# Nyström attention on one core: another order of the work between the pseudoinverse products, on TensorE, VectorE and ScalarE

## What is computed

```python
k = split_heads(x @ Wk); q = split_heads(x @ Wq) / math.sqrt(HS); v = split_heads(x @ Wv)   # 16 heads of 16
q_l = q.reshape(B, H, M, denom, HS).sum(axis=-2) / denom          # 64 landmarks
k_l = k.reshape(B, H, M, denom, HS).sum(axis=-2) / denom
s1 = softmax(einsum('bhld,bhmd->bhlm', q, k_l))
s2 = softmax(einsum('bhmd,bhnd->bhmn', q_l, k_l))
s3 = softmax(einsum('bhmd,bhld->bhml', q_l, k))
z = s2.T / (col * row)            # col, row: the largest sums of |s2|
for _ in range(6):
    xz = s2 @ z
    z = 0.25 * z @ (13 * I - xz @ (15 * I - xz @ (7 * I - xz)))
out = (s1 @ (z @ (s3 @ v))) @ Wo + bo
```

## Time and profile before

| | us |
|---|---|
| median of 3 runs | 1236.3 |
| lowest and highest | 1235.24, 1238.79 |
| the profiled execution | 1237.7 |
| its span | 1235.9 |
| of that: TensorE busy | 1125.6 (91%) |
| VectorE, ScalarE, GpSimd busy | 750.7, 595.1, 544.3 |

### The profile page before, as it was taken

One profiled execution on the slowest core, in us unless ns is written; L12 is line 12 of the kernel. 1 busy time (PEld: TensorE's weight loads), 2 busy tenths in 40 slices (PEclk: granted clock), 3 DMA queues, 4 the chain that ended last, 5 costly groups with the idle time before them and its releaser, 6 DMA issues.

```text
span 1235.9 us, 29651 instructions
## 1 busy us (share of the span) xinstructions
PE 1125.6 (91%) x11140; PEld 915.5 (74%) x11141; DVE 750.7 (61%) x1391; ACT 595.1 (48%) x953; POOL 544.3 (44%) x634
## 2 busy tenths in 40 slices
PE   7899889999999378899999998989999888999997
PEld 6677678888887266677777776868887677888786
DVE  5536346766665466757668666655445346667664
ACT  5433235666664345354444554525443335666663
POOL 2131544666665624333534342234204535665674
PEclk8899899999999789999999999999999999999999
DMA  7173214222210300000000000011453032221220
GB/s 239 34 263 137 95 49 163 66 69 69 66 56 28 119 19 3 2 3 2 3 2 3 2 4 3 3 36 69 154 188 103 18 120 71 65 63 58 69 68 18
DMA packets 42030, 80.45 MB, mean 65 GB/s; under 512 B 9012, under 2 KB 33719, under 8 KB 40896
## 3 DMA queue, kind: packets, MB, share of 16 engines
q1 hardware_dynamic: 28640, 53.62, 12.3%
q0 software_dynamic: 13280, 25.27, 6.8%
HBM read 57.21 MB, written 27.15 MB: 68 GB/s over the span
## 4 chain that ended last, share of the span: by engine, by line
PE 68%; DVE 16%; ACT 6%; issue 6%; DMA 2%; POOL 1%; another core or an unknown queue 1%; DVEq 0%; ACTq 0%; POOLq 0%; SPq 0%
PE PS L1596 16%; PE PS L1610 10%; PE PS L1522 8%; PE PS L1539 6%; PE PS L1784 4%; PE PS L1677 3%; PE PS L1797 3%; PE PS L1603 3%; DVE A_NM L722 2%; DVE A_NM L729 2%; PE PS L1459 2%; PE PS L1546 2%; PE PS L1747 1%; PE PS L1818 1%; PE PS L1721 1%
## 5 line engine op out<-in xcount | busy, mean ns | idle before, releaser
L1596 PE MATMUL PS<-WHL,XGH 128*128 128x512 f32 x624 | 217.0, 429 | 3.5 <-DVE WHL L604 3.4
L1610 PE MATMUL PS<-WD,XNT 128*128 x624 | 149.9, 383 | 1.5 <-ACT XNT L1063 1.5
L1373 POOL TENSOR_TENSOR A_A<-A_XC,A_ST 128x320 f32<-128x320 f32 (+1 forms) x96 | 73.7, 781 | 172.2 <-ACT A_ST L1129 171.6
L625 DVE SCALAR_TENSOR_TENSOR XNT<-PS,WHO,XNT 128x512 f32<-128x512 f32 x78 | 58.3, 748 | 120.5 <-PE PS L1596 104.1
L1596 PEld LDWEIGHTS PS<-WHL,XGH 128*128 128x128 f32 x624 | 111.3, 189 | 22.6 <-issue 2.7
L1058 ACT ACTIVATE XNT<-PS,WHO 128x512 f32<-128x512 f32 x78 | 53.7, 688 | 148.7 <-PE PS L1596 135.5
L1277 POOL DMA_INDIRECT who_dram<-TOK,SLOT x64 | 66.1, 1033 | 132.7 <-issue 108.7
L1539 PE MATMUL PS<-SDH,HHL 128*128 128x256 f32 x512 | 108.0, 294 | 18.2 <-DVE X L551 15.8
L1610 PEld LDWEIGHTS PS<-WD,XNT 128*128 128x128 f32 x624 | 112.6, 190 | 15.9 <-issue 2.0
L1596 PE MATMUL PS<-WHL,XGL 128*128 128x512 f32 x312 | 123.1, 395 | 0.0
L1282 POOL DMA_INDIRECT X<-xs_dram,WHO x78 | 99.5, 1276 | 51.2 <-issue 26.5
(11 more groups left out here) (256 smaller groups left out, 2548.9 us busy)
## 6 DMA issues: line engine op xcount, KB each, us to landing
xs_dram<-WG SPq DMA_DIRECT2D x16, 512.0 KB, 2.9
WU<-in_r_up SPq DMA_DIRECT2D x2, 4096.0 KB, 13.9
shared_dram<-X SPq DMA_DIRECT2D x16, 512.0 KB, 3.1
WG<-in_r_gate SPq DMA_DIRECT2D x2, 4096.0 KB, 16.9
WD<-in_r_down SPq DMA_DIRECT2D x4, 2048.0 KB
X<-in_x SPq DMA_DIRECT2D x8, 512.0 KB, 9.3
X<-mid_dram SPq DMA_DIRECT2D x8, 512.0 KB, 3.8
X<-xs_dram,WHO POOLq DMA_INDIRECT x78
```

What stands on the lines that cost most here:

```text
L625: dve.scalar_tensor_tensor(B["RH"][:, u * F:(u + 1) * F], banks[3 + u][:], score(t), B["RS"][:, u * F:(u + 1) * F], ALU.mult, ALU.mult).th ...
L1373: pool.tensor_tensor(a, x, st, ALU.add).then_inc(att["a"], 1)
L1596: ins = pe.matmul(banks[bank][:], tok, w[:, k * F:(k + 1) * F], start=(k == 0 and i == 0), stop=(k == KD - 1 and i == 2))
L1610: ins = pe.matmul(banks[7][:, 0:D], B["HT"][:, u * F + f * P:u * F + (f + 1) * P], B["WD"][:, bass.ds(ex * (KF * D) + f * D, D)], start=(f ...
```

## The change

No operation is added or taken away; blocks move between gaps, a few waits and PSUM banks go with them.

- TensorE: `denominators(old)` goes from step 2 to step 0, behind `heads(old, 1)`. In step 2, `turn_nm3` and `project_qk(far, 0)` now lead. `project_v(nxt, 1)` comes ahead of `s1_turned(b, 0)`. `project_qk(far, 1)` stands ahead of the first product of step 4, `project_qk(far, 2)` and `s1_max(nxt, 0)` ahead of the second; the column sums (now the function `column_sums`) and `s1_max(nxt, 1)` go ahead of the first product of step 5, `project_qk(far, 3)` and `turn_sums` ahead of its second. `start_t` comes before `turn_nm1`.
- VectorE: both key landmarks of `far` are reduced at the end of the round, the reciprocal of the denominators comes in step 0, `add_projection(done, 0)` behind `chain_x(b, 1)`, `s1_max(nxt, 0)` ahead of `chain_x(b, 4)`, the second `s1_max` in two halves around `chain_b(b, 5)`, and `start_t` ahead of `chain_x(b, 5)`.
- ScalarE: `numerators` is split, its first half stands ahead of `chain_s(b, 0)`; the copies follow the projections.
- Banks: `project_qk` uses 6, 6, 6, 7 in place of 7, 6, 6, 6; `project_v` 6 and 7 in place of 6 and 6; `turn_nm1` 7 in place of 6; the column sums and `turn_sums` 6 in place of 7.

```diff

@@ -860,8 +861,9 @@
         if b == NG - 1:
             first_rows(1)
         if exists(nxt):
-            landmarks(nxt, 1, 1)
             s3_max(nxt, 0)
+        if exists(old):
...
             key_block(nxt)
@@ -874,28 +876,25 @@
             low_tokens(far, 1)
         if exists(nxt):
             s2_shift(nxt)
+        chain_x(b, 1)
         if exists(done):
             add_projection(done, 0)
-        chain_x(b, 1)
         if exists(nxt):
             s2_sum(nxt)
+        chain_b(b, 2)
         if exists(ln):
             batch_stats(ln)
...
-        if exists(ln):
             batch_aggregate(ln)
...
         if exists(nxt):
             key_rows(nxt)
-        if exists(old):
-            denominators(old)
         chain_x(b, 2)
+        if exists(nxt):
+            row_sums(nxt)
         if exists(far):
             landmarks(far, 0, 0)
-        if exists(nxt):
-            row_sums(nxt)
@@ -912,28 +911,30 @@
             heads_norm(old)
         if exists(nxt):
             row_kept(nxt)
+            s1_max(nxt, 0, (0, 1))
         chain_x(b, 4)
         if exists(nxt):
-            s1_max(nxt, 0)
+            column_max(nxt)
+            s1_max(nxt, 1, (0,))
         chain_b(b, 5)
         if b == NG - 1:
             denominators(b)
         if exists(nxt):
-            s1_max(nxt, 1)
-            column_max(nxt)
+            s1_max(nxt, 1, (1,))
...
             first_scale()
+        if exists(nxt):
+            start_t(nxt)
+        chain_x(b, 5)
         if exists(far):
             landmarks(far, 0, 1)
-        chain_x(b, 5)
+            query_block(far)
+        if exists(nxt):
+            start_y(nxt)
+            product_kept(nxt)
         if exists(far):
-            query_block(far)
             landmarks(far, 1, 0)
-        if exists(nxt):
-            start_t(nxt)
-            start_y(nxt)
-        if exists(nxt):
-            product_kept(nxt)
@@ -1163,9 +1164,11 @@
     for b in PERIODS:
         old, nxt, far, ln = b - 1, b + 1, b + 2, b + 3

+        if exists(old):
+            numerators(old, 0)
         chain_s(b, 0)
         if exists(old):
-            numerators(old)
+            numerators(old, 1)
...
+        chain_s(b, 2)
+        if exists(nxt):
             act.wait_ge(att["nm3_ready"], count("nm3_ready", nxt, 1))
             act.copy(B["NM3T"][:], banks[7][:, 0:P]).then_inc(att["nm3"], 1)
-        chain_s(b, 2)
-        if exists(nxt):
-            exp3(nxt, 0)
         if exists(far):
             projected(far, 0)
+            rounded(far, 0)
+        if exists(nxt):
+            exp3(nxt, 0)
+            values(nxt, 1)
         if exists(b):
             exp1(b, 0)
-        if exists(far):
-            rounded(far, 0)
-        if exists(nxt):
+        chain_s(b, 3)
+        if exists(nxt):
+            sums_kept(nxt, 0)
             act.wait_ge(att["kbd"], count("kbd", nxt, 1))
             act.copy(B["KBDR"][:], B["KBD"][nxt % 2][:]).then_inc(att["bdr"], 1)
-        if exists(nxt):
-            values(nxt, 1)
-        chain_s(b, 3)
-        if exists(nxt):
-            sums_kept(nxt, 0)
             exp3(nxt, 1)
         if exists(b):
             exp1(b, 1)
+        if exists(far):
+            projected(far, 1)
         chain_s(b, 4)
         if exists(far):
-            projected(far, 1)
             rounded(far, 1)
-        if exists(nxt):
-            sums_kept(nxt, 1)
+            projected(far, 2)
+            rounded(far, 2)
...
+        if exists(nxt):
+            sums_kept(nxt, 1)
...
         chain_s(b, 5)
         if exists(far):
-            projected(far, 2)
-            rounded(far, 2)
-        if exists(far):
             projected(far, 3)
             act.wait_ge(att["qbd"], count("qbd", far, 1))
             act.copy(B["QBDR"][:], B["QBD"][:]).then_inc(att["bdr"], 1)
         if exists(nxt):
             act.wait_ge(att["nm1_ready"], count("nm1_ready", nxt, 1))
-            act.copy(B["NM1T"][:], banks[6][:]).then_inc(att["nm1"], 1)
@@ -1838,23 +1843,27 @@
         if exists(old):
             pe.wait_ge(att["ws"], count("ws", old, 1))
             pe.wait_ge(att["e1"], count("e1", old, 4))
-            pe.wait_ge(att["nm1"], count("nm1", b, 1))
-            pe.wait_ge(att["rec"], count("rec", old - 1, 1))
+            pe.wait_ge(att["tm"], count("tm", b, 1))
             heads(old, 0)
         chain_first(b, 0)
         if exists(old):
-            pe.wait_ge(att["tm"], count("tm", b, 1))
+            pe.wait_ge(att["nm1"], count("nm1", b, 1))
             pe.wait_ge(att["xo"], count("xo", old - 2, 2))
             heads(old, 1)
+            if b == 1:
+                pe.wait_ge(s_picks, 5)
+            pe.wait_ge(att["num"], count("num", old, 1))
+            denominators(old)

         chain_second(b, 0)
         if exists(far):
             pe.wait_ge(att["xn"], count("xn", far, GT))
             pe.wait_ge(att["num"], count("num", old, 2))
-            pe.wait_ge(att["tm"], count("tm", b, 1))
+            pe.wait_ge(att["nm1"], count("nm1", b, 1))
             pe.wait_ge(att["qk"], count("qk", nxt, 4))
             turn(far, 0)
-            pe.wait_ge(att["nm1"], count("nm1", b, 1))
+            pe.wait_ge(att["tm"], count("tm", b, 1))
+            pe.wait_ge(att["rec"], count("rec", old, 1))
             turn(far, 1)
@@ -1879,43 +1888,39 @@
...
+            pe.wait_ge(att["rec"], count("rec", old, 1))
             project_v(nxt, 0)
+
+        chain_first(b, 2)
+        if exists(nxt):
             pe.wait_ge(att["xo"], count("xo", done, 1))
+            pe.wait_ge(att["s3m"], count("s3m", nxt, 4))
             turn_nm3(nxt)
-
-        chain_first(b, 2)
+        if exists(far):
+            pe.wait_ge(att["xtl"], count("xtl", far, 2))
+            pe.wait_ge(att["v_sb"], count("v_sb", nxt, 1))
+            if far == 0:
+                pe.wait_ge(s_low, 4)
+            project_qk(far, 0)
         if exists(nxt):
             if b == -1:
                 pe.wait_ge(s_picks, 5)
             pe.wait_ge(att["nm3"], count("nm3", nxt, 1))
             pe.wait_ge(att["s2s"], count("s2s", nxt, 1))
             s3_turned(nxt, 0)
-        if exists(old):
-            if b == 1:
-                pe.wait_ge(s_picks, 5)
-            pe.wait_ge(att["num"], count("num", old, 1))
-            pe.wait_ge(att["xtl"], count("xtl", far, 2))
-            pe.wait_ge(att["v_sb"], count("v_sb", nxt, 1))
-            denominators(old)
-        if exists(far):
-            pe.wait_ge(att["xtl"], count("xtl", far, 2))
+
+        chain_second(b, 2)
+        if exists(nxt):
             pe.wait_ge(att["nm3"], count("nm3", nxt, 1))
-            if far == 0:
-                pe.wait_ge(s_low, 4)
-            project_qk(far, 0)
-
-        chain_second(b, 2)
+            project_v(nxt, 1)
         if exists(b):
             pe.wait_ge(att["nm1"], count("nm1", b, 1))
             pe.wait_ge(att["e3"], count("e3", nxt, 2))
             s1_turned(b, 0)
-        if exists(nxt):
-            pe.wait_ge(att["v_sb"], count("v_sb", nxt, 1))
-            pe.wait_ge(att["rec"], count("rec", old, 1))
-            project_v(nxt, 1)
...
         chain_first(b, 3)
         if exists(nxt):
+            pe.wait_ge(att["qk"], count("qk", far, 1))
             pe.wait_ge(att["v_sb"], count("v_sb", nxt, 2))
@@ -1924,8 +1929,7 @@
             pe.wait_ge(att["e1"], count("e1", b, 2))
             s3_turned(nxt, 1)
         if exists(done):
-            pe.wait_ge(att["qk"], count("qk", far, 1))
-            pe.wait_ge(att["nm3"], count("nm3", nxt, 1))
+            pe.wait_ge(att["v_sb"], count("v_sb", nxt, 2))
             pe.wait_ge(att["xo"], count("xo", done, 1))
             project(done, 1)
@@ -1936,9 +1940,13 @@
             s1_turned(b, 1)
         if exists(nxt):
             pe.wait_ge(att["rsum"], count("rsum", nxt, 1))
+            pe.wait_ge(att["v_sb"], count("v_sb", nxt, 2))
             pe.wait_ge(att["xo"], count("xo", done, 2))
+            turn_rows(nxt)
+        if exists(far):
+            pe.wait_ge(att["tts"], count("tts", nxt, 1))
             pe.wait_ge(att["qk"], count("qk", far, 1))
-            turn_rows(nxt)
+            project_qk(far, 1)
@@ -1949,22 +1957,24 @@
             pe.wait_ge(att["rmax"], count("rmax", nxt, 2))
             spread_rows(nxt)
         if exists(far):
-            pe.wait_ge(att["tts"], count("tts", nxt, 1))
-            pe.wait_ge(att["xtl"], count("xtl", far, 2))
-            project_qk(far, 1)
-
-        chain_second(b, 4)
+            pe.wait_ge(att["qk"], count("qk", far, 2))
+            project_qk(far, 2)
         if exists(nxt):
             pe.wait_ge(att["ot"], count("ot", old, 2))
             pe.wait_ge(att["e3"], count("e3", nxt, 4))
             pe.wait_ge(att["qkr"], count("qkr", nxt, 2))
             pe.wait_ge(att["bdr"], count("bdr", nxt, 2))
             s1_max(nxt, 0)
+
+        chain_second(b, 4)
+        if exists(nxt):
             pe.wait_ge(att["rs"], count("rs", nxt, 1))
             pv(nxt, 1)
-        if exists(far):
```

(27 more changed lines are left out.)

58 lines of the change are left out of this document (32 added, 26 removed).

## The result

The changed kernel takes 1220.63 us (median of four, 1219.25 to 1224.01), the kernel before 1237.55 beside it (1235.24 to 1243.82): ratio 0.9851 [0.9823, 0.9879], or 16.9 us less. On another chip it was 1219.71 against 1238.38, ratio 0.9836 [0.9789, 0.9884]. The profiled execution took 1224.01, with a span of 1222.2.

What follows compares the result with a forecast made beforehand. TensorE was taken to bound the kernel, with only idle time to win; gains of 11.8 + 3.0 + 1.8 - 0.2 - 0.3 + 0.3 = 16.4 us took the median from 1236.3 to 1220, range 1213 to 1231.

Steps and rivals of the forecast that it cites:

- Denominators to step 0: Steps 0 and 1: moving the denominators removes waits of 0.16, 0.46 and 0.34 us, gaining 0.96 a full round.
- Second product of step 1: Step 1: VectorE's path comes 1.0 us earlier, TensorE's 0.80, so at most 0.1 of the 0.19 wait is left.
- `add_projection`: Before step 2's first product: moved behind XC on VectorE, it gains 0.19 us, with 0.1 to spare.
- `project_v(nxt, 1)`: Step 3: its copy, put ahead of `exp1(b, 0)` on ScalarE, removes the 0.49 us wait before `pv`.
- `project_qk(far, 1)`: Step 4: put ahead of the first product, it covers the 0.66 us wait for `exp1(b, 1)` before `spread_denominators`.
- Step 4: Second product put behind `s1_max(nxt, 0)`, which needs the heads' normalisation: an added wait costing 0 to 0.1 us.
- Step 5: End of the round: VectorE's `start_t` goes ahead of XC and other work, removing TensorE's 0.58 us wait before `start_t`.
- Rival 4: More than counted: round 7's slow clock goes, same-shape blocks side by side save 0.3 us a round; 1216 us, chance 0.09.
- Clock: Round 7's slow stretch, about 1.6 us, counted as staying; it might go (1218.5) or come twice (1221.5).
- the forecast's own case: Nearly all TensorE idle time in full rounds goes; a total of 1216.5 to 1224 us, chance 0.62.
- Rival 1: Waits come back at thin places in steps 1, 2 and 4, losing 8 us of the gain: 1228 us, chance 0.18.
- Rivals 2 and 3: VectorE becomes the bound in steps 4 and 5, 1247 us, chance 0.05; idle is not real slack, 1236, chance 0.06.

Runs made afterwards that it cites:

- the kernel with step 4 put back: Changed kernel with `s1_max(nxt, 0)` behind step 4's second product and its maxima behind `chain_x(b, 4)`: full rounds 48.06 us; 1205.22 us in all, on another chip.
- the kernel with only round 7 altered: Changed kernel with only round 7's denominators back in step 2: round 7 34.64 us, round 6 46.87; 1203.58 us in all, on another chip.
- the undone version: Changed kernel with the denominators back in step 2 in every round: 50.84, 50.82 and 51.24 us in rounds 2 to 4, 49.34 in round 5.
- The experiment with the end of the round: Changed kernel with TensorE's last product, `turn_sums`, `start_y`, `turn_nm1` and `start_t` ordered as before: full rounds 47.97 us, 0.57 more than in the changed kernel.

## Why the prediction was right, and where it was not

The forecast of 1220 stands against 1220.6, and the reason holds: TensorE bounds a full round, its idle time was real slack, and nearly all of it went. That the two totals agree to 1 us is partly luck. The sum hid errors that went both ways: 3.7 us of gain that it left out in the full rounds, and 6.6 us of loss that it left out in round 7 and the fill. The traces account for 13.0 of the 16.9 us. Each term is set against the mean of two executions of each kernel, and then against executions at the same clock, where there are such. By content round 7 lost 0.6 us less and the fill 0.6 more than the table says, since `turn_nm1` changed sides of the cut:

| gain, us | forecast | mean of two | both at clock 1.00 |
|---|---|---|---|
| rounds 2 to 5 | 11.8 | 15.5 | 15.5 |
| round 1 | 3.0 | 3.4 | 3.5 |
| round 0 | 1.8 | 1.1 | 1.85 |
| round 6 | -0.2 | -0.4 | -0.3 |
| round 7 | -0.3 | -3.7 | -0.7 |
| fill | +0.3 | -2.9 | not seen |
| sum | 16.4 | 13.0 | |

For round 7 at clock 1.00 the 33.35 us of the kernel with step 4 put back are set against the 32.61 of before. For round 1 at clock 1.00 the row of the kernel with only round 7 altered is used, whose round 1 is that of the changed kernel (us, TensorE busy, granted clock):

```profile
503.43:550.24 46.81, 44.04 (x898) 1.00 0.01 3
```

**Denominators to step 0 (0.96).** Right, and close to the count. From the first product's start (609.75 in the changed kernel) the second product was forecast at 4.15 and came at 4.00, the reciprocal's end at 5.5 and came at 5.47, XC at 6.4 and came at 6.26. What the count left out is the bank that the later projection shares; the undone version showed that.

**Second product of step 1 (at most 0.1 left of 0.19).** Wrong: all 0.19 stayed. VectorE's low tokens had begun 1.20 us after `turn` ended; now they begin at 616.32, `turn` having ended at 616.03, so 0.29 after: a gain of 0.91, not the 1.0 I took. TensorE's way from `turn` to the product shrank by 0.91 too (4.97 to 4.06, both without the wait), not by the 0.80 of its waits, since its blocks became shorter. A race of two paths that both got shorter by the same amount ends as before.

**`add_projection` (0.19).** Right; the margin is 0.30, not 0.1. I had called it the thinnest place; that is the second product of step 1, which has less than none.

**`project_v(nxt, 1)` (0.49) and `project_qk(far, 1)` (0.66).** Both waits went, alone and together with the rest. Alone the second earned 0.42, since it uncovers 0.39 elsewhere; the forecast had it beside the moves that fill that place.

**Step 4 (0 to 0.1 lost).** Right that nothing is lost, but the term's sign in the full change is a gain: without the move, 0.66 comes back. I had judged it by its own gap and not by the maxima that a later block waits for.

**Step 5 (0.58).** Right. The wait stays away when TensorE's order at the end of the round is put back, so TensorE's order is not what removed it.

**The term that was mis-sized.** The step that failed is "The change removes no work, so idle time is all that it can win in rounds 2 to 5", and with it a full round of 48.2 to 48.5 us and TensorE's busy time "unchanged at 48.1": the round is 47.40, with 47.2 busy. The idle time gave 2.88 a round and the blocks themselves 0.99. Rival 4 named this mechanism with 0.3 us a round. Put together from the starts of neighbouring blocks, less the waits: `turn_nm3` in front of a projection 0.08 where it took 0.28 in front of a waiting 64*64 product, `turn_rows` 0.02 in place of 0.20, `heads(old, 1)` 0.88 in place of 1.06, `start_y` 0.96 for 1.08, the last product 0.96 for 1.04, `project_qk(far, 3)` 1.49 for 1.61, and 0.05 to 0.07 for each of several blocks whose successor had had to wait; against them the column sums take 0.22 more and `project_v(nxt, 0)` 0.08. The first of these as rows of the kernel before and of the changed one:

```profile
624.91 0.27 PE L1707 MATMUL PS<-CB,A_NM 128*128 128x128 f32 x1
625.38 1.32 PE L1784 MATMUL PS<-A_XC 64*64 64x80 f32 x32 [0.19 <-DVE A_XC L818]
```

```profile
624.41 0.33 PE L1709 MATMUL PS<-CB,A_NM 128*128 128x128 f32 x1
624.49 0.48 PE L1679 MATMUL PS<-A_XTH,A_WQH 128*128 128x512 f32 x1
```

625.38 less the wait of 0.19 is 0.28 after the transpose's start; in the changed kernel the projection begins 0.08 after it. The experiment with the end of the round shows the effect by itself (some 0.4 us of its 0.57); for the blocks of the other steps it is read from the two traces, and not tried one by one. Why one neighbour costs more than another is open.

**Clock.** "It may go (1218.5) or come twice (1221.5); I count it as staying" was too kind for the profiled execution. The lower level appeared in four places of the profiled execution: the fill (0.75, against 0.84 before), rounds 0 and 1 (0.96), the end of round 6 (0.96) and round 7 (0.87). In round 7, 0.13 x 37.8 = 4.9 us of full clock are missing, against 0.05 x 34.15 = 1.7 before, so that the round without them is near 33 in both kernels. That is an estimate, as the granted clock is a mean that counts idle time too; measured at 1.00 are 33.35 with the changed order and 32.61 before. The order of the last rounds was forecast well (-0.2 and -0.3; at clock 1.00, with `turn_nm1` counted on one side, -0.3 and -0.1); the clock was not. The Trainium skill, "TensorE: Matmul & The Clock Gate", Part 1, ties the clock to how busy TensorE has just been. The profiled execution agrees, with products of 2.40 and 2.17 us just behind idle stretches of 1.42 and 1.14 and none of over 1.32 in the four full rounds; the second execution has the same stretches and products of 1.32, so one idle stretch does not say what the clock does.

**The rivals.** Of the five, the forecast's own case held, with rival 4's second half on top of it at three times its size. Rival 1 (waits come back at thin places) held at one place, 0.19. Rivals 2 and 3 fell: VectorE is busy 36.0 us of 47.4, and the blocks as a whole became shorter, though two stretched (0.22 and 0.08).

**What stays open.** The profiled attention became 8.9 us shorter in the first pair and 13.0 on the mean of two each, and the medians moved 16.9 and 18.7. Since the full rounds repeat, the difference must lie outside them: in the clock of the partial rounds of executions that have no trace, or in the spread of the parts ahead of and behind the attention. Neither was settled.

## What to carry to other kernels

Before blocks are moved between the waits of a bound engine, count three things for each move: the wait it covers, the wait it uncovers, and who shares its bank or buffer at the new place. A move that earns nothing at its own place can be what lets another stand. Blocks have no fixed length either: 0.99 us a round came from which block follows which and from blocks whose successor no longer has to wait. Treat filling and draining rounds as kernels of their own: an order that suits the full round left gaps of 1.1 to 1.4 us in rounds 6 and 7, and giving these rounds and the fill their own order and banks brought the median from 1219.7 to 1213.1. And compare partial rounds at the same granted clock, over several traces, before an order is held to be the cause: 1.7 to 3.1 us that seemed to come from the denominators' place in round 7 were 0.2 at the same clock.

## What the runs showed of the hardware

- TensorE's own stream depends on its neighbours: the same five blocks, with the same instructions, took 4.18 us (4.31 less 0.13 idle) in one order and 3.84 in another, with the 64*64 blocks side by side (up to 0.07 of the difference can belong to the wait).
- The same code gets its higher clock at different times. In the fill, eight traces with the same two waits (0.78 and 0.69) reached the upper level (2.4 in place of 1.2 GHz; 0.39 us in place of 0.63 for a matmul of 512 columns) 3.7 to 11.7 us after the first projection, and the four projections took 9.05 to 12.55 us.
- Full rounds of one order repeated to 0.05 us on every chip, while rounds 0, 1, 6 and 7, which have idle stretches of about 1 us, differed by up to 2.7 us between two executions of the same kernel, together with the granted clock (50.35 us at 1.00, 53.07 at 0.94).
- An idle stretch of 1.42 us was followed by a product of 2.40 us in one execution and of 1.32 in another of the same kernel.
- The trace's "issue" can hide a wait: 0.66 us before `spread_denominators` went away when work was put ahead of it. And a wait of 0.13 us can stand there without a bracket.
